# Layer 1's last passes of a two-layer decoder: the feed-forward pass in f32 instead of three bf16 parts, and seven tiles' follow-up work inside the shared attention pass instead of four

## What is computed

```python
x = layernorm(x + xattn(x, ctx))   # q, k, v and the probabilities are quantised; all 1024 queries see all 1024 keys, 16 heads of 16
# out = (attn @ v) ; xattn = out @ Wp + bp
x = layernorm(x + ffn(x))
# wq = fp8_e4m3(w); gate = silu((x @ wq_gate) * s_gate); up = (x @ wq_up) * s_up
# ffn = ((gate * up) @ wq_down) * s_down      (256 -> 768 -> 256)
```

## Time and profile before

| | |
|---|---|
| median of 3 runs | 1430.68 us (1428.68 to 1430.94) |
| the profiled execution | 1430.41 us, its span 1428.6 us |
| PE, DVE, ACT, POOL busy | 90%, 73%, 48%, 9% of the span |
| shared pass (first to last maximum) | 1145.6 to 1345.3 us |
| after it, to the end of the span | 83 us |

### The profile page before, as it was taken

One profiled execution on the slowest core, in us unless ns is written; L12 is line 12 of the kernel. 1 busy time (PEld: TensorE's weight loads), 2 busy tenths in 40 slices (PEclk: granted clock), 3 DMA queues, 4 the chain that ended last, 5 costly groups with the idle time before them and its releaser, 6 DMA issues.

```text
span 1428.6 us, 24438 instructions
## 1 busy us (share of the span) xinstructions
PE 1287.9 (90%) x9113; PEld 854.0 (60%) x9113; DVE 1050.0 (73%) x2349; ACT 680.0 (48%) x1286; POOL 135.1 (9%) x223
## 2 busy tenths in 40 slices
PE   6979999999999999999999999988999689998886
PEld 3747667766766766766676676656777423332344
DVE  5768578588578667857857765744888788888687
ACT  2336335434534633643543463432444287788641
POOL 2210010020011011001001000000000011111101
PEclk9989999999999999999999999999999755555598
DMA  7331002000100100200200023002000089899800
GB/s 237 153 104 62 12 12 66 12 5 12 62 12 16 62 11 16 62 12 5 73 12 1 12 62 118 20 23 97 8 9 5 1 142 168 151 167 175 145 1 30
DMA packets 174789, 83.96 MB, mean 59 GB/s; under 512 B 137936, under 2 KB 170064, under 8 KB 174416
## 3 DMA queue, kind: packets, MB, share of 16 engines
q1 hardware_dynamic: 173520, 82.03, 23.7%
q10 hardware_dynamic: 1152, 0.36, 0.1%
HBM read 43.57 MB, written 5.24 MB: 34 GB/s over the span
## 4 chain that ended last, share of the span: by engine, by line
PE 65%; DVE 19%; issue 6%; ACT 5%; DMA 4%; POOL 1%; ACTq 0%; DVEq 0%; POOLq 0%
PE ps_t L1886 12%; PE ps_p L1870 11%; PE ps_s L2119 8%; PE ps_o L2036 5%; PE ps_o L2026 4%; PE ps_o L1951 4%; PE ps_o L2119 3%; DMA w_moe<-w_moe 3%; PE ps_p L1928 3%; DVE w_moe L1764 3%; DVE probs L1261 2%; PE ps_s L1928 2%; PE ps_o L1955 2%; DVE row_max L1267 2%; PE ps_t L2379 1%
## 5 line engine op out<-in xcount | busy, mean ns | idle before, releaser
L1886 PE MATMUL ps_t<-ident,probs 128*128 128x128 f32 x1072 | 169.8, 280 | 28.5 <-ACT probs L1044 8.0
L904 ACT ACTIVATE probs<-probs 128x512 f32<-128x512 f32 x184 | 115.6, 628 | 136.6 <-DVE probs L1261 136.6
L1886 PEld LDWEIGHTS ps_t<-ident,probs 128*128 128x128 f32 x1072 | 122.9, 141 | 78.1 <-issue 37.9
L866 ACT ACTIVATE probsT<-ps_t 128x512 f32<-128x512 f32 x232 | 136.5, 589 | 62.8 <-PE ps_t L1886 62.6
L2119 PE MATMUL ps_s<-w_moe,xbT 128*128 128x352 f32 x352 | 123.6, 476 | 0.0
L1870 PE MATMUL ps_p<-w_qkv,xinT 128*128 128x512 f32 (+1 forms) x240 | 106.5, 568 | 10.2 <-DMA xinT<-in_xT 6.8
L2393 PEld LDWEIGHTS ps_p<-vals,w_moe 128*128 128x128 f16 x1024 | 37.7, 106 | 116.5 <-DMA w_moe<-w_moe 77.2
L809 POOL TENSOR_TENSOR rms<-mean_sq,neg_half 128x8 f32<-128x8 f32 x40 | 67.1, 1679 | 269.4 <-DVE mean_sq L1295 269.4
L866 ACT ACTIVATE bigT<-ps_t 128x512 f32<-128x512 f32 (+1 forms) x128 | 68.9, 553 | 33.2 <-PE ps_t L1886 31.2
L2119 PEld LDWEIGHTS ps_s<-w_moe,xbT 128*128 128x128 f32 x352 | 64.7, 196 | 22.6 <-issue 2.3
L1951 PE MATMUL ps_o<-v_all,probsT 128*128 128x128 f32 x512 | 70.6, 282 | 6.7 <-DVE big L1325 6.2
(11 more groups left out here) (344 smaller groups left out, 2683.9 us busy)
## 6 DMA issues: line engine op xcount, KB each, us to landing
w_out<-in_wT_out SPq DMA_DIRECT2D x8, 2048.0 KB, 8.5
w_moe<-in_wT_gu SPq DMA_DIRECT2D x1, 5632.0 KB, 17.8
w_moe<-in_wT_down SPq DMA_DIRECT2D x1, 2816.0 KB, 10.1
keys<-keys2T SPq DMA_DIRECT2D x8, 256.0 KB, 2.0
keys2T<-keys SPq DMA_DIRECT2D x1, 2048.0 KB, 10.3
w_moe<-w_moe SPq DMA_TRANSPOSE x128, 3.3
w_qkv<-in_wT_qkv SPq DMA_DIRECT2D x3, 512.0 KB, 5.0
w_qkv<-in_wT_qkv SPq DMA_DIRECT2D x1, 1536.0 KB, 8.3
```

Source lines behind the costliest of these rows:

```text
L866: nc.scalar.activation(dst, src.bitcast(BF16) if dst.dtype == BF16 else src, ACT.Copy)\
L904: nc.scalar.activation(probs[:, at % 4, :], probs[:, at % 4, :], ACT.Exp).then_inc(L0.exped, 1)
L1886: ins = nc.tensor.transpose(dst[:, i * P:(i + 1) * P], src(i), ident_b[:] if bf else ident[:])
```

## The change

Four things. (1) The third pass multiplies f32 activations with f32 weights: `gate_and_up` is 4 products of 512 columns, `down` 6 of 256, and every split into bf16 parts goes (`x5_first` to `x5_last`, `fuse_first` to `fuse_last`). The turned tile is copied once by ACT (`x5_take`). (2) The weights are rounded in place, in f32. (3) The companions run inside the shared pass for tiles 0 to 6; only tile 7 has them after it. (4) The first six blocks use the shared pass's three pairs of banks in its rotation, so `gate_and_up(0)` waits for the exponentials of unit 125 only, and block b < 6 for block b-3. The scores of the shared pass are computed as before.

```diff
@@ companions (OQ_TURN, OQ_TAKE, IN5 and OUT5 likewise)
-X5_TURN, X5_FIRST, X5_REST, X5_SECOND, X5_LAST = 0, 1, 3, 4, 6
+X5_TURN, X5_TAKE = 0, 1
-                if 1 <= t <= HT and h == OUT2:
+                if 1 <= t <= LAST and h == OUT2:
                     out_project(t - 1)
-                if 2 <= t <= HT + 1 and h == X5_TURN:
+                if 2 <= t <= TILES and h == X5_TURN:
                     x5_turn(t - 2)
@@ block_banks
-            return ps_s if b % 2 == 0 else ps_o
+            return shared_scores(TILES * H1 - 3 + b) if b < IB else (ps_s, ps_o)[b % 2]
@@ ScalarE
-            def x5_first(n):
...
+            def x5_take(n):
                 act.wait_ge(x5_turned, n + 1)
+                nc.scalar.activation(x5T[n // HT][:, n % HT, :], tile_bank(n), ACT.Copy).then_inc(x5_taken, 1)
...
+            x5_take(LAST - 1)
+            for b in range(2 * IB):
+                gate(b)
+                if b == 1:
+                    oq_take(LAST)
+                if b == 4:
+                    x5_take(LAST)
@@ VectorE, after the shared pass
             gate_up_block(0)
             take_shared(LAST)
             gate_up_block(1)
             gate_up_block(2)
             in5(LAST)
             gate_up_block(3)
             out5(LAST)
             gate_up_block(4)
             gate_up_block(5)
             for b in range(IB, 2 * IB):
-                d = b - IB - 3
+                d = b - IB - 2
@@ TensorE
             def gate_and_up(b):
                 half, j = b // IB, b % IB
                 if j == 0:
-                    pe.wait_ge(parts5, HT * (half + 1))
-                if b >= 2:
-                    pe.wait_ge(fused, b - 1)
+                    pe.wait_ge(x5_taken, HT * (half + 1))
+                if b < 3:
+                    pe.wait_ge(exp2, HEADS - 2 + b)
                 else:
-                    pe.wait_ge(exp2, HEADS - 1 + b)
+                    pe.wait_ge(fused, b - 2 if b < IB else b - 1)
                 for i, w in ((0, w_gate1), (1, w_up1)):
                     for k in range(KD):
-                        for part in range(3):
-                            ins = nc.tensor.matmul(block_banks(b)[:, i, :], w[:, k, j * P:(j + 1) * P],
-                                                   x5p[:, part, k, half * HALF:(half + 1) * HALF],
-                                                   start=(k + part == 0), stop=(k == KD - 1 and part == 2))
+                        ins = nc.tensor.matmul(block_banks(b)[:, i, :], w[:, k, j * P:(j + 1) * P],
+                                               x5T[half][:, :, k * P:(k + 1) * P], start=(k == 0),
+                                               stop=(k == KD - 1))
...
                 if u == HEADS:
-                    pe.wait_ge(exp2, HEADS - 2)
-                    out_turn(HT)
-                    out_turn(HT + 1)
-                if u == HEADS + 1:
-                    out_project(HT)
-                if u == HEADS + 2:
-                    out_turn(HT + 2)
                     gate_and_up(0)
...
             def down_blocks(d, psum, blocks):
-                    pe.wait_ge(fparts, b + 1)
-                    for part in range(3):
-                        ins = nc.tensor.matmul(psum, fusep[b][:, part, d % HT * P:(d % HT + 1) * P], w_down1[:, j, :],
-                                               start=(j + part == 0), stop=(j == IB - 1 and part == 2))
+                    pe.wait_ge(fused, b + 1)
+                    ins = nc.tensor.matmul(psum, fuses[b][:, d % HT * P:(d % HT + 1) * P], w_down1[:, j, :],
+                                           start=(j == 0), stop=(j == IB - 1))
...
             gate_and_up(1)
             out_turn(LAST)
             gate_and_up(2)
             out_project(LAST)
             gate_and_up(3)
             x5_turn(LAST)
             gate_and_up(4)
             gate_and_up(5)
             gate_and_up(IB)
             gate_and_up(IB + 1)
             for b in range(IB + 2, 2 * IB):
                 gate_and_up(b)
                 down(b - IB - 2)
```

More of the change, by code:

```diff
@@ L365, in decoder @@
         ffn_gate, ffn_up = over.take(KD * I1), over.take(KD * I1)
+        w_gate1, w_up1 = (w.rearrange("p (k n) -> p k n", k=KD) for w in (ffn_gate, ffn_up))
+        turned_at = over.at
         round_low, round_high = over.take(PIECE // 2, dt=BF16), over.take(PIECE // 2, dt=BF16)
@@ L368, in decoder @@
         round_two = over.take(PIECE, dt=BF16)
-        over = Region(w_x[:].rearrange("p a b -> p (a b)"))
-        w_gate1 = over.take(KD, I1, dt=BF16)
-        w_up1 = over.take(KD, I1, dt=BF16)
+        x5T = [w[:, at:at + HT * D].rearrange("p (t n) -> p t n", t=HT) for w, at in
+               ((w_x[:].rearrange("p a b -> p (a b)"), 0), (w_out0[:].rearrange("p a b -> p (a b)"), turned_at))]
         over = Region(w_moe)
@@ L583, in decoder @@
         x5_turned = sem("x5_turned")
[L584 to L587, removed]
+        x5_taken = sem("x5_taken")
         gate_up1 = sem("gate_up1")
@@ L625, in decoder @@
         ffn_down = flat(ropes[:])
[L628 to L633, removed]
+        w_down1 = ffn_down.rearrange("p (k n) -> p k n", k=IB)
+        homes = [Region(keys2T[:].rearrange("p a b c -> p (a b c)").bitcast(F32)), Region(turn_words)]
+        fuses = [homes[b // 8].take(HALF) for b in range(2 * IB)]
+        tts, gs = squares, probs[:, 0:2, :]
         N4, N5, N6 = (Norms(sem, f"_{n}", *zip(*((r, rest.take(6), rest.take(2), rest.take(1)) for r in pair)))
@@ L637, in decoder @@
         assert nv1 >= (H1 - 1) * (HD1 + 1) + WIDE
-        for used in (rest, freed, outs, keys, dups, free, *homes):
+        for used in (rest, outs, keys, dups, free, *homes):
             assert used.at <= used.ap.shape[-1]
@@ L841, in _ @@
                                         ALU.add).then_inc(max2_ready, 1)
-                if 1 <= t <= HT and h == IN5:
+                if 1 <= t <= LAST and h == IN5:
                     power1(N5, t - 1)
-            for t in range(HT, TILES):
-                power1(N5, t)
+            power1(N5, LAST)
             for t in range(TILES):
@@ L1097, in _ @@
                                      accum_out=q2s[:, 3, h:h + 1]).then_inc(exp2, 1)
-                if 1 <= t <= HT and h == OQ_TAKE:
+                if 1 <= t <= LAST and h == OQ_TAKE:
                     oq_take(t - 1)
[L1100 to L1103, removed]
+                if 2 <= t <= LAST and h == X5_TAKE:
+                    x5_take(t - 2)
             def gate(b):
@@ L1110, in gate @@
                                      scale=scales1[:, 2, b % IB:b % IB + 1]).then_inc(tanhed1, 1)
[L1112 to L1118, removed]
-            act.wait_ge(scaled_scales, 1)
[L1121 to L1156, removed]
+            act.wait_ge(scaled_scales, 1)
+            x5_take(LAST - 1)
[5 more added lines that the diff above has]
+                    x5_take(LAST)
         @block.vector
@@ L1766, in _ @@
                     take_shared(t - 1)
-                if 1 <= t <= HT and h == IN5:
+                if 1 <= t <= LAST and h == IN5:
                     in5(t - 1)
-                if 1 <= t <= HT and h == OUT5:
+                if 1 <= t <= LAST and h == OUT5:
                     out5(t - 1)
-                if 2 <= t <= HT + 1 and h == X5_REST:
-                    x5_rest(t - 2)
-                if 2 <= t <= HT + 1 and h == X5_LAST:
-                    x5_last(t - 2)
             def gate_up_block(b):
@@ L2434, in last_blocks @@
                 return down_blocks(d, last_sums(d), blocks)
-            x5_turn(HT)
-            out_project(HT + 2)
             gate_and_up(1)
-            x5_turn(HT + 1)
             out_turn(LAST)
@@ L2442, in _ @@
             out_project(LAST)
-            x5_turn(HT + 2)
             gate_and_up(3)
+            x5_turn(LAST)
             gate_and_up(4)
-            x5_turn(LAST)
             gate_and_up(5)
```

80 lines of the change are left out of this document (7 added, 73 removed).

## The result

The changed kernel takes 1434.4 us (median of 8 runs, 1430.55 to 1435.95) against 1428.2 us of the kernel before (8 runs, 1427.08 to 1431.02): the ratio on record is 1.0036, 95% interval 1.0025 to 1.0047 (the quotient of the two medians alone is 1.0043). It is slower, as forecast, and 1434.4 lies inside the range of 1432.5 to 1442.5; the predicted 1438.0 was 3.6 us too high. The profiled execution took 1433.95 us, its span 1432.2.

A forecast was written before the change was run, and what follows sets the result against it. Bounds: half-clock PE, DVE and ACT all too busy in the shared pass; afterwards PE, first waiting for DVE, with DVE-bound norms at the end. +8.3 - 0.7 = +7.6 us on 1430.41 gave 1438.0 us, range 1432.5 to 1442.5.

The forecast's parts named there:

- The shared pass, +8.3 us: Shared pass, tiles 5 to 7: three more companion sets cost 5.5 us in tiles 5 and 6, 2.8 in tile 7.
- bound of the transposes: Shared pass: cost 5 us if the transposes catch up during the stall, 10 us if they fall behind.
- Splits, first pass, rounding in f32: 0: Splits leaving tiles 2 to 5 give back nothing (at most 3.3 us); first-pass rounding costs nothing (at most 4.9 us).
- Products: Third pass on PE: f32 gate block 3.44 us instead of 2.59, down 2.58 instead of 1.96.
- The third pass, -0.7 us: Third pass: a gain of 0.7 us, slower products taking what the waits of before cost.
- the four sums: Third pass on PE: sums 124 to 127, queued behind gate 0, 0.47 us each, 1.9 us together.
- half clock cost block 0: Start of the third pass: gate block 0 begins at half clock and loses 2.6 us (bounds 1.7 and 3.4).
- the wait: Third pass, after gate block 3: PE idle 2.9 us at x5_turn(7), which needs out5(7) from DVE.
- the clock fell behind it: Third pass, after PE's idle at x5_turn(7): a possible half-clock stretch costing 1.7 us, half taken, 0.85.
- the faster case: Rival, chance 0.06: the clock rises in the shared pass, saving 8.3 us there and 2.6 at gate 0; 1427.1 us.
- The slower one: Rival, chance 0.12: later clock rise in gate 0, more half clock after x5_turn(7)'s wait, transposes behind; 1442.2 us.
- the case without a change: Rival, chance 0.12: splits leaving tiles 2 to 5 and transposes catching up in tiles 5 to 7 give 3.3 us each; 1431.4.

The follow-up runs named there:

- e6: Changed kernel with out_project of the companions multiplying bf16 copies of both operands instead of f32; 1425.80 us, ratio 0.9975 to the kernel before.
- e5: Kernel before, third pass still in three bf16 parts, with the changed kernel's placement (companions of tiles 0 to 6 inside the shared pass); 1430.63 us, ratio 1.0010.
- e2: Changed kernel with 10 extra unused bf16 products on TensorE ahead of tile 7's x5_turn; 1433.18 us, ratio 1.0031 to the kernel before.
- e3: Changed kernel with the last four tiles' down sums each done whole, tile after tile; 1429.81 us, ratio 1.0019 to the kernel before.
- e1: Changed kernel with tile 7's x5_turn after gate block 4 instead of ahead of it; 1429.69 us, ratio 1.0013 to the kernel before.
- e8: Changed kernel with the edits of e1 and e3 together; 1425.08 us, ratio 0.9974 to the kernel before.
- e10: e4 with the whole downs of e3 and the work of tiles 4 to 7 after the shared pass reordered; 1426.12 us, ratio 0.9967 to the kernel before.
- e7: Changed kernel with out_project's two products issued in two different units and later companion steps one unit later; 1433.83 us, ratio 1.0028 to the kernel before.
- e9: Changed kernel with the first six blocks on two pairs of banks in turn again; 1436.62 us, ratio 1.0044 to the kernel before.
- e4: Changed kernel, f32 third pass kept, with the old placement (only companions of tiles 0 to 3 inside the shared pass); 1433.87 us, ratio 1.0041 to the kernel before.

## Why the prediction was right, point by point

- **The shared pass, +8.3 us.** It was 7.7. Tiles 5 and 6 came at 26.12 and 26.07 against 26.37, tile 7 at 25.08 against 25.30. Pricing a set by whole tiles, waits included, was the step that held; e6 shows about half of it to be `out_project` in f32 at half clock (1.33 of some 2.6 us a set). Neither bound of the transposes (5 and 10 us) came.
- **Splits, first pass, rounding in f32: 0.** Tiles 1 to 4 take 105.98 us against 105.48, so the splits that left them gave nothing back. Ahead of the pass nothing shows beyond the spread between executions, so a small cost of the rounding can't be told: the pass begins at 1145.6 us in both bf16 traces and at 1140.5 to 1147.7 in the f32 ones.
- **Products.** A block took 3.43 (3.44 predicted) and a down 2.59 (2.58), the strided x5 included. A bf16 product of 512 columns keeps its 0.216 us in e5 as well. The Trainium skill (TensorE: Matmul & The Clock Gate, Back-to-back issue gap) states a sustained 131 ns for it; no run here shows that, and the measurement decides.
- **The third pass, -0.7 us.** It was -2.6, and this is the largest error of the mechanism. Term by term: block 0 starts 0.6 us behind the start of the last maximum instead of 1.8 (-1.2). With companions in tile 7, PE issued the last scores 2.8 us ahead of their maximum (1347.49 and 1350.26), before 1.1 us. The prediction had said that nothing there waits on DVE; PE in fact waits 1.34 us for `out5(6)`, and the earlier start hid that. Further: the four sums took 0.79 instead of 1.9, as the 0.47 of one was the time of its weight loads, not its share of a stream (-1.1); half clock cost block 0 5.45 - 3.44 = 2.0 instead of 2.6 (-0.6), which is partly luck, as block 0 took 5.0 to 6.4 us in the timelines with f32 and seven sets (5.65 in that of the changed kernel); the wait was 2.61 instead of 2.9 (-0.3); the clock fell behind it for certain, 1.7 instead of the half I took (+0.85). That makes the first of the last norms come 3.1 us earlier than before, 1420.55 - 1350.26 = 70.3 against 73.4. The end then took 11.65 us instead of 11.1, as all four norms now follow at 2.13 us.
- **The sum's reference.** Most of the 3.6 us is not mechanism: the eight runs have the kernel before at 1428.2, and I started from a profiled execution at 1430.41, 2.2 us higher. Of the change itself I forecast +7.6 us. The medians give +6.2, the ratio +5.1 (0.36% of 1428.2), and the two stages in the traces +7.7 - 2.6 = +5.1. So the mechanism was 1.4 to 2.5 us off, in the same direction as the reference.
- **The rivals.** The clock did not rise in the shared pass in any of these kernels (0.50 in every trace), so the faster case had no ground. The slower one had one of its parts, the fall at the wait, for which e2 is the test. Of the case without a change, neither the splits nor the transposes gave anything back.
- **What I did not see.** I called the norms at the end unchanged and bound by DVE. Their spacing was (2.13 us each), but their start was set by the order of PE's products: e3 takes 5.2 us from there. And I priced the wait at tile 7's turn without noting that the change itself had moved the turn ahead of block 4; e1 puts it back.

## What to carry to other kernels

A term can be priced right and still leave money in the schedule. After a change of what binds a stage, look again at every order that was made to hide the old bound (here the split of the last sums), and at every place where the change itself put a step that waits ahead of one that doesn't (here a turn ahead of a block); the two were worth 9.3 us together. A comparison of two ways to compute in one inherited order is also a comparison of how well the order fits each. Work that is put beside a loop costs its own length if the engine that paces the loop does it, and more than where it came from if that engine's clock is at half there. Three bf16 products were cheaper for TensorE than one f32 product, 0.65 against 0.86 us for 512 columns. In the inherited order f32 lost by that; in the order of e8 and e10 the f32 kernels beat the bf16 kernel before, and whether a bf16 kernel with a new order would beat them is open.

## What the runs showed of the hardware

An idle of 2.61 us on TensorE was followed by 3.41 us at half clock in the changed kernel, e3, e6, e7 and e9; in e2, where ten products of no use fill it, by none. The same stretch costs 1.7 us of a dense block. I had put the fall at one in two. The length of the idle does not decide by itself: one of 2.05 us was followed by such a stretch in e4 and by none in the kernel before, where one of 3.02 us was followed by none either.

In the shared pass PE was busy for 89% of the time (184.43 of 206.15 us in the changed kernel), and the granted clock stayed at 0.50 in all twelve traces.
